# Differential attention in 16 groups: one unrolled sequence, three score banks, maxima of two heads at once

## The reference

```python
qkv = x @ Wqkv                                     # x: normalised and modulated rows
q = qkv[..., :2 * Hx].reshape(Bx, 2 * NQ, Sx, HD)  # 32 query heads of 16, Sx = 2048
k = qkv[..., 2 * Hx:2 * Hx + G].reshape(Bx, NKV, Sx, HD)   # 8
v = qkv[..., 2 * Hx + G:].reshape(Bx, NKV, Sx, HD)
k = jnp.repeat(k, 2 * NQ // NKV, axis=1)
v = jnp.repeat(v, NQ // NKV, axis=1)
scores = jnp.einsum('bhqd,bhkd->bhqk', q, k) / math.sqrt(HD)
scores = jnp.where(causal, scores, -jnp.inf)
aw = jax.nn.softmax(scores, axis=-1)
aw = aw.reshape(Bx, NQ, 2, Sx, Sx)
aw = aw[:, :, 0] - lam * aw[:, :, 1]
attn = jnp.einsum('bhqk,bhkd->bhqd', aw, v) * (1.0 - LAMBDA_INIT)
```

## Time and profile before

| | |
|---|---|
| median of three runs | 2430.19 us (2429.91 to 2431.61) |
| the profiled execution | 2430.3 us |
| its span, first to last instruction | 2428.4 us |
| TensorE busy | 2220.2 us, 91% |
| VectorE busy | 1829.4 us, 75% |
| ScalarE busy | 1547.9 us, 64% |
| GpSimd busy | 525.7 us, 22% |
| granted TensorE clock, mean | 0.949 |

### The profile page before, as it was taken

How to read it: one execution, slowest core, us unless ns; L and a number is a source line. 1 busy time by engine, 2 the same in 40 slices (tenths; PEclk the granted TensorE clock), 3 DMA queues, 4 the chain that set the end, 5 groups by cost and what they waited for, 6 DMA issues and landing times. The chain is left out here.

```text
span 2428.4 us, 46606 instructions
## 1 busy us (share of the span) xinstructions
PE 2220.2 (91%) x17772; PEld 992.5 (41%) x17772; DVE 1829.4 (75%) x3782; ACT 1547.9 (64%) x3105; POOL 525.7 (22%) x584
## 2 busy tenths in 40 slices
PE   6799999999999999999999999999999979889984
PEld 4233333333333333333333333334333258567831
DVE  2788888878787888888888888887888348434467
ACT  2167677777767776767676777777767725235633
POOL 2112121303222121212121213131201014100067
PEclk8589999999999999999999999999999979899955
DMA  4120302121121202020303030212100030000001
GB/s 145 36 58 6 66 11 61 22 50 32 41 41 31 47 25 47 30 56 17 66 6 66 6 66 18 55 27 45 32 12 2 2 96 0 1 1 1 1 22 48
DMA packets 95990, 84.79 MB, mean 35 GB/s; under 512 B 48544, under 2 KB 81440, under 8 KB 95776
## 3 DMA queue, kind: packets, MB, share of 16 engines
q1 hardware_dynamic: 95776, 81.91, 15.2%
HBM read 26.81 MB, written 16.78 MB: 18 GB/s over the span
## 5 line engine op out<-in xcount | busy, mean ns | idle before, releaser
L605 DVE TENSOR_REDUCE m_part<-a_bank 128x1 f32<-128x512 f32 (+3 forms) x2560 | 1395.5, 603 | 270.0 <-PE a_bank L906 163.2
L749 ACT ACTIVATE probs<-b_bank 128x512 f32<-128x512 f32 (+1 forms) x2304 | 1173.2, 578 | 412.4 <-PE b_bank L922 407.2
L922 PE MATMUL b_bank<-q_pack,k_pack 34*128 34x512 bf16 (+7 forms) x5120 | 949.0, 348 | 6.2 <-DMA q_pack<-m_rows 1.8
L894 PE MATMUL a_bank<-k_pack,q_pack 64*128 64x512 bf16 (+3 forms) x2560 | 847.2, 357 | 58.5 <-DVE m_part L605 33.0
L960 PE MATMUL acc<-probs,v_tile 128*32 128x512 f32 (+3 forms) x5120 | 587.1, 540 | 22.6 <-ACT o_sb L756 21.5
L922 PEld LDWEIGHTS b_bank<-q_pack,k_pack 34*128 34x128 bf16 (+1 forms) x5120 | 316.5, 94 | 547.7 <-ACT probs L749 392.6
L894 PEld LDWEIGHTS a_bank<-k_pack,q_pack 64*128 64x128 bf16 x2560 | 238.2, 94 | 333.4 <-DVE m_part L605 255.2
L476 POOL TENSOR_SCALAR_AFFINE_SELECT probs<-probs 128x512 f32<-128x512 f32 (+1 forms) x192 | 151.5, 789 | 1019.4 <-ACT probs L749 1019.4
L906 PE MATMUL a_bank<-future,pick 64*128 64x128 bf16 x2048 | 278.3, 219 | 0.0
L906 PEld LDWEIGHTS a_bank<-future,pick 64*128 64x128 bf16 x2048 | 185.7, 96 | 47.5 <-issue 4.7
L960 PEld LDWEIGHTS acc<-probs,v_tile 128*32 128x32 f32 x5120 | 107.3, 108 | 186.6 <-issue 94.2
(11 more groups left out here) (193 smaller groups left out, 1761.0 us busy)
## 6 DMA issues: line engine op xcount, KB each, us to landing
q_pack<-part SPq DMA_DIRECT2D x384, 64.0 KB, 2.3
k_pack<-part SPq DMA_DIRECT2D x192, 64.0 KB, 2.3
scratch<-qkv_row SPq DMA_DIRECT2D x16, 512.0 KB, 2.8
heads<-scratch SPq DMA_DIRECT2D x16, 512.0 KB, 3.7
xg<-in_L_attn_x SPq DMA_DIRECT2D x16, 256.0 KB, 2.8
scratch<-qkv_row SPq DMA_DIRECT2D x32, 128.0 KB, 2.7
q_pack<-m_rows SPq DMA_DIRECT2D x256, 2.0 KB
x<-in_L_attn_x SPq DMA_DIRECT2D x4, 1024.0 KB, 11.7
```

Of the source, the lines that this page charges most:

```text
L605: dve.tensor_reduce(m_part[:, 2 * hp + side, t, c:c + 1], a_bank[at % A_RING][:, 0:width_a(u % UNITS)], AX.X, ALU.max).then_inc(a_maxed, 1)
L749: act.activation(probs[:, s % P_RING, h, at:C], b_bank[bank_no(("B", par, s, h))][:, at:C], ACT.Exp, scale=HD ** -0.5) \
L894: ins = pe.matmul(a_bank[at % A_RING][:, 0:w], q_pack[buf][rows, hp, 0, q:q + P], k_pack[buf][rows, 0, C * c:C * c + w], start=True, stop= ...
L922: ins = pe.matmul(b_bank[bank_no(slot)][:, at:at + C - q], k_pack[par][rows, n2, P * kt:P * (kt + 1)], q_pack[par][rows, h // 2, n2, C * j ...
```

## The change

- One list over all 16 x 36 steps (TAIL steps with three more at the end) takes the place of the list for two groups. The flush is gone: the last two `meet_v` of a group fall into steps 0 and 1 of the next, the copy of `acc` into step 1 and piece O into step 2.
- `b_bank` has three banks. The slots of a step are now h0, h1, extra pieces, h2, h3. The extra pieces stand between the two `two_heads`, on TensorE behind `meet_v` and on ScalarE between the exponentials of h1 and h2; so do ScalarE's copies.
- `a_bank` has two pairs of banks. A unit waits for the reduction of the unit two before it; VectorE reduces both heads in one instruction, when both are scored. The masks of a unit with fewer than 512 columns come one score earlier.
- The output: ScalarE copies the turned rows to `o_rows`, VectorE takes reciprocal and signs one step later, GpSimd scales and adds.
- VectorE's negation of a block's maxima is spread over the next two units; piece M comes one step later; T0 to T3 come one step later; the gather of heads goes from VectorE (step 15) to GpSimd (step 14).

```diff
...
 SIDES = (1, 0)
-A_RING = 3
-B_RING = 4
+A_RING = 2
+B_RING = 3
...
-PREP_AT = {7: "N", 8: "W0", 9: "W1", 10: "W2", 11: "W3", 17: "T0", 18: "T1", 19: "T2", 20: "T3"}
...
+PREP_AT = {7: "N", 8: "W0", 9: "W1", 10: "W2", 11: "W3", 18: "T0", 19: "T1", 20: "T2", 21: "T3"}
+COPY_AT = {STEPS * g + J_LAST[j] + LAG: 4 * g + j for g in range(GROUPS) for j in range(NJ)}
+OUTPUT_AT = {n + 1: block for n, block in COPY_AT.items()}
+MAXIMA_AT = {n + 2: 4 * (u // UNITS) + A_LAST.index(u % UNITS)
+             for n in range(LAST_STEP) for u in units(n) if u % UNITS in A_LAST}
+GATHER_AT = 14
...
-SLOTS = [slot for par in range(2) for s in range(STEPS)
-         for slot in [("B", par, s, h) for h in range(QH)] + [(use, par, s, 0) for use in MISC[s]]]
-SLOTS[-1:-1] = [None] * (-len(SLOTS) % B_RING)
+TAIL = LAST_STEP + LAG + 1
+USES = [use for n in range(TAIL) for use in uses_at(n)]
+SLOTS = [slot for n in range(TAIL)
+         for slot in [("B", n, h) for h in range(QH // 2) if n < LAST_STEP] + uses_at(n)
+         + [("B", n, h) for h in range(QH // 2, QH) if n < LAST_STEP]]
+SLOT_NO = {slot: at for at, slot in enumerate(SLOTS)}
...
-        a_bank = [ps(f"a_bank{i}", [P, C]) for i in range(A_RING)]
+        a_bank = [ps(f"a_bank{i}", [P, 2, C]) for i in range(A_RING)]
         b_bank = [ps(f"b_bank{i}", [P, C]) for i in range(B_RING)]
...
+            def gather_heads(n):
+
+                pool.wait_ge(heads_in, 32 * (n + 1))
+                pool.wait_ge(turned, 4 * n)
+                pool.tensor_copy(heads_by_j[:, :, :, :], heads[:, :, :].rearrange("p h (j d) -> p j h d", d=HD)) \
+                    .then_inc(heads_ready, 1)
...
+            def pair(n):
+
+                g, j = n // NJ, n % NJ
+                o = o_sc[:, :].rearrange("p (t h e) -> p t h e", t=TB, h=QH)
+                halves = o_sc[:, :].rearrange("p (t a c e) -> p t a c e", t=TB, a=2, c=2)
+                dst = attn[:, g, TB * j:TB * (j + 1), :].rearrange("p t (a e) -> p t a e", a=2)
+                pool.wait_ge(o_weighed, n + 1)
+                if n:
+                    pool.wait_ge(o_added, n)
+                pool.tensor_tensor(o, o_rows[:, :].rearrange("p (t h e) -> p t h e", t=TB, h=QH)[:, :, :, 0:HD],
+                                   o_w[:, :, :].unsqueeze(3).broadcast_to([P, TB, QH, HD]), ALU.mult).then_inc(o_scaled, 1)
+                pool.wait_ge(o_scaled, n + 1)
+                pool.tensor_tensor(dst, halves[:, :, :, 0, :], halves[:, :, :, 1, :], ALU.add).then_inc(o_added, 1)
...
-            def maximum(i, par, u):
+            def maximum(u):

                 j, t, c, hp = A_UNITS[u % UNITS]
-                for n, side in enumerate(SIDES):
-                    at = 2 * a_count(i, par, u) + n
-                    dve.wait_ge(a_scored, at + 1)
-                    dve.tensor_reduce(m_part[:, 2 * hp + side, t, c:c + 1], a_bank[at % A_RING][:, 0:width_a(u % UNITS)],
-                                      AX.X, ALU.max).then_inc(a_maxed, 1)
-
-            def negate(i, par, u, j, m):
-
-                dve.wait_ge(a_maxed, 2 * a_count(i, par, u) + 2)
-                dve.tensor_reduce(m_max[:, :, :], m_part[:, :, :, 0:j + 1], AX.X, ALU.max).then_inc(m_step, 1)
-                dve.wait_ge(m_step, upto(2 * m + 1))
-                if not (isinstance(m, int) and m == 0):
-                    dve.wait_ge(m_copied, upto(m))
+                dve.wait_ge(a_scored, 2 * u + 2)
+                dve.tensor_reduce(m_part[:, j % 2, 2 * hp:2 * hp + 2, t, c], a_bank[u % A_RING][:, :, 0:width_a(u % UNITS)],
+                                  AX.X, ALU.max).then_inc(a_maxed, 1)
...
-            def weigh(i, par, last, s, j):
-
-                n = 4 * (2 * i + par) + j
-                o = b_bank[bank_no((f"O{j}", par, s, 0))][:, :].rearrange("p (t h e) -> p t h e", t=TB, h=QH)
-                dve.wait_ge(misc_filled, upto(misc_no(i, par, last, s, f"O{j}")))
-                dve.reciprocal(o_rl[:, :, :], o[:, :, :, HD]).then_inc(o_step, 1)
-                dve.wait_ge(o_step, upto(2 * n + 1))
-                dve.tensor_tensor(o_w[:, :, :], o_rl[:, :, :], signs[:, :, :], ALU.mult).then_inc(o_step, 1)
-                dve.wait_ge(o_step, upto(2 * n + 2))
-                dve.wait_ge(o_added, upto(START + n - (1 if par or j else 0)))
-                dve.tensor_tensor(o_sc[:, j % 2, :].rearrange("p (t h e) -> p t h e", t=TB, h=QH), o[:, :, :, 0:HD],
-                                  o_w[:, :, :].unsqueeze(3).broadcast_to([P, TB, QH, HD]), ALU.mult).then_inc(o_scaled, 1)
...
+            def invert(n):
+
+                dve.wait_ge(o_taken, n + 1)
+                if n:
+                    dve.wait_ge(o_scaled, n)
+                dve.reciprocal(o_rl[:, :, :], o_rows[:, :].rearrange("p (t h e) -> p t h e", t=TB, h=QH)[:, :, :, HD]) \
+                    .then_inc(o_inverted, 1)
+
+            def weigh(n):
+
+                dve.wait_ge(o_inverted, n + 1)
+                dve.tensor_tensor(o_w[:, :, :], o_rl[:, :, :], signs[:, :, :], ALU.mult).then_inc(o_weighed, 1)
...
-            def body(i, last):
-                for par in range(2):
-                    g = 2 * i + par
-                    for s in range(STEPS):
-                        exponentials(i, par, s)
-                        for j in range(NJ):
-                            if s == J_LAST[j] + LAG or s == STEPS - 1 == J_LAST[j]:
...
+            def take_rows_of_output(block, no, bank):
+                act.wait_ge(misc_filled, no)
+                if block:
+                    act.wait_ge(o_added, block)
+                act.activation(o_rows[:, :], bank[:, :], ACT.Copy).then_inc(o_taken, 1)
+
+            for n in range(TAIL):
+                if n < LAST_STEP:
+                    for h in range(QH // 2):
+                        exponential(n, h)
+                if n in COPY_AT:
+                    take_output(COPY_AT[n])
+                for use in uses_at(n):
+                    (what, k), no, bank = use, use_no(use), b_bank[bank_no(use)]
+                    if what == "N":
+                        shift_rows(k, no, bank)
+                    if what == "W":
+                        take_rows(k // 4, k % 4, no, bank)
+                    if what == "T":
+                        take_heads(k // 4, k % 4, no, bank)
+                    if what == "M":
+                        take_maxima(k, no, bank)
+                    if what == "O":
+                        take_rows_of_output(k, no, bank)
+                    if what == "T" and k % 4 == 3:
+                        first_part(k // 4)
+                if n < LAST_STEP:
+                    for h in range(QH // 2, QH):
+                        exponential(n, h)
         @block.tensor
...
+            def wait_for_bank(slot):
+
+                if SLOT_NO[slot] >= B_RING:
+                    was = SLOTS[SLOT_NO[slot] - B_RING]
+                    if was[0] == "B":
+                        pe.wait_ge(b_exped, START + QH * was[1] + was[2] + 1)
+                    else:
+                        emptied(*was)
...
-                at = 2 * a_count(i, par, u) + n
                 rows = slice(HALF * side, HALF * (side + 1))
-                if at >= A_RING:
-                    pe.wait_ge(a_maxed, at - A_RING + 1)
-                ins = pe.matmul(a_bank[at % A_RING][:, 0:w], q_pack[buf][rows, hp, 0, q:q + P], k_pack[buf][rows, 0, C * c:C * c + w],
+                if n == 0 and u >= A_RING:
+                    pe.wait_ge(a_maxed, u - A_RING + 1)
+                ins = pe.matmul(a_bank[u % A_RING][:, side, 0:w], q_pack[buf][rows, hp, 0, q:q + P], k_pack[buf][rows, 0, C * c:C * c + w],
...
-            def body(i, last):
-                for par in range(2):
-                    g = 2 * i + par
-                    for s in range(STEPS):
-                        j = B_STEPS[s][0]
-                        if s == J_FIRST[j]:
-                            pe.wait_ge(m_rows_in, upto(16 * QH * (4 * g + j + 1)))
-                        ahead = [u for u in units(s) if not (last and par == 1 and u >= UNITS)]
-                        ending = s == STEPS - 1
-                        pieces = 2 + (LAG if ending else 0)
-
...
-                        if UNITS in ahead:
-                            pe.wait_ge(packs_in, 16 * PACK_DMAS * (g + 2))
-                        two_heads(i, par, s, 0, maxima(0), last)
-                        if s >= LAG:
-                            meet_v(i, par, s - LAG)
-                        two_heads(i, par, s, 1, maxima(1), last)
-                        if ending:
-                            for k in range(LAG):
-                                for u in maxima(2 + k):
-                                    score_maxima(i, par, u)
...
+            for n in range(TAIL):
+                g, s = n // STEPS, n % STEPS
+                ahead = list(units(n)) if n < LAST_STEP else []
+                if n < LAST_STEP and s in J_FIRST:
+                    pe.wait_ge(m_rows_in, 16 * QH * (NJ * g + J_FIRST.index(s) + 1))
```

(59 more changed lines are left out.)

343 lines of the change are left out of this document (138 added, 205 removed).

## The result

The changed kernel takes 2534.6 us (median of four, 2533.3 to 2537.2), the kernel before 2430.05 in the same batch: a ratio of 1.0426, 95% interval 1.0411 to 1.0442. It is slower by 104 us; forecast were 72, in a range that held it. The profiled execution took 2533.4 us, its span is 2531.7 at a mean granted clock of 0.947 (before: 0.949).

The account below looks back on a forecast made before the run. TensorE was taken to set the pace at 2.50 us a step, VectorE close behind. 14 groups x 4.4 + 2 + 10 - 3 + 1 gave +72 on 2430.3, so 2502 us; range 2395 to 2560, one in ten beyond each end.

Parts of the forecast that it names:

- the price that decides: Three score banks, not four: h1's scores wait for the exponential of h2, plain steps 2.82 us instead of 2.50.
- Rival (a): Faster: the three-bank loop is not felt, -3.6 us a group, 2375 us; chance 0.12.
- Rival (b): Faster: VectorE sets the time and 1280 fewer reductions count in full, 2390 or 2248 us; chance 0.08.
- (d): Nothing moves: the flush and copies give what the loop costs, 2425 to 2435 us; chance 0.07.
- Rival (c): Slower still: later rows and paired reductions feed each other's waits, 122.5 to 123 a group, 2550 to 2560 us; chance 0.15.
- Group 15 longest in relation: Sign in the profile after: the last group, 92.03 us before, would take 102.1, +10.
- A gap of 2 us after the split: Sign in the profile after: TensorE idle 2 us behind ScalarE's 1.91 us split.
- the wait for the rows: Step 10 waits for its maxima rows: some 4.5 us in group 14, 0.6 to 0.7 in a group with preparation.
- Cost 0; were that cover gone, T0 would wait 1 to 2 us: Moving the output's rescaling and the gather of heads from VectorE to GpSimd would cost nothing.
- the pairs of maxima: Units waiting for paired reductions hold up h1 after steps with three or four units: 3.5 us a group.
- A TensorE that waits mainly for the paired reductions: Sign in the profile after that would show the forecast wrong; no size given.
- The lead: The 46 units ahead of the loop, VectorE's alone, would get 3 us shorter.

Follow-up runs that it names:

- the best kernel: Changed kernel with four score banks, three single maxima banks, GpSimd's split held until step 27's exponentials, maxima rows ahead of pack transfers: 2398.9 us, ratio 0.9860.

## Why the prediction was right, and where its sum was off

**Right: the price that decides.** The loop 1.29 + 0.22 + 0.32 + 1.00 was forecast at 2.82 a step, and it is 2.82 in the changed kernel, in the old one with three banks, and in the new one with single maxima banks; 2.50 with four; 2.61 with half of h2's exponential. Rival (a), in which the loop is not felt, is out. Rival (b) is out by the 142 us less of VectorE that brought nothing, and (d) by 104 us. Rival (c), 2550 to 2560, came nearer to 2534.6 than the 2502 did, but not by its causes: no wait for rows in a usual group, and little cost of the pairs. "Group 15 longest in relation": 12%, forecast 102.1, measured 103.7. "VectorE below 90": 88.0. "A gap of 2 us after the split" on ScalarE: the score behind it waits 1.82 us:

```profile
1416.23 1.91 ACT L718 ACTIVATE part<-headT 80x2048 bf16<-80x2048 f32 x1
...
1418.67 0.39 PE L913 MATMUL b_bank<-q_pack,k_pack 64*128 64x512 bf16 x1 [1.82 <-ACT probs L746]
```

**Right in group 14: the wait for the rows.** Forecast 4.5, measured 3.8 at step 10, which took 7.37 there (before: 1.84). The group as a whole came out at 114.6 and not 110.4: behind the wait the granted clock was 0.58 from 1859.90 to 1866.19 us, a cost that the sum did not have. The answer on the bank's loads (idle us, times):

```profile
  DMA q_pack<-m_rows: 3.8, 1
```

The 0.7 us forecast for each other group (its own times, 33.8 less 33.3, give 0.5) did not show in group 10: step 10 was 0.57 shorter than forecast. I had the time of arrival and the time of need each to a microsecond, and their difference is no better than that.

**Off: a usual group +6.7 to +7.2, not +4.4.** In group 10 the steps come to 121.6, 2.2 above the forecast (119.4 with its steps rounded one by one):

- Step 26, +1.0 in five of the groups. The failing sentence is "Cost 0; were that cover gone, T0 would wait 1 to 2 us". I asked only who waits for the rescaling on GpSimd and not what the signs' product, still on VectorE, meets there. The product runs into the split, and the reductions stand behind it. The kernel before had shown 0.92 for a product of 0.17.
- In the other nine groups step 26 is as forecast and the loss sits in steps 22 and 23, 9.33 us in group 8 for 8.14 in group 10 (some 8.3 by the prediction's terms). The sum had the gap behind the split on ScalarE, and nothing for what the gap can do to the granted clock, which falls to 0.51 behind it.
- Steps 3, 21 and 19, +1.6 (0.88, 0.56, 0.18). The negation, spread over two more units, comes late, and TensorE's turn of maxima waits for it, 21.1 us in all, where the kernel before shows one wait of 0.4. I costed it at nothing and never named its cover. The wait in step 3:

```profile
1350.55 0.22 PE L827 MATMUL b_bank<-identb,m_neg 128*32 128x128 bf16 x1 [0.72 <-DVE m_neg L607]
```

- Steps 30 and 6, +0.46, with no cause followed up.
- Against these steps 10, 20 and 2, -1.2: the rows' wait and ScalarE's copies were overestimated there.
- The rest is spread over steps at 0.1 to 0.3 each.

**Right sum, wrong ground: the pairs of maxima.** The steps for which I put down 3.5 us came out within 0.2 each, yet single maxima banks give nearly the same steps. So the pairs' own price was mis-sized: 0.9 us for four steps and not 2.95. With single maxima these four steps take the same with three score banks as with four (4.49, 3.36, 3.14, 3.50), so what is left in them is the third unit itself, on TensorE and VectorE, which no run separates. "A TensorE that waits mainly for the paired reductions" was to prove me wrong and does not appear: 166.4 + 78.3 us of loads and matmuls, where the single ones had 255.2 + 33.0 before:

```profile
PEld a_bank L882 <- DVE m_part L589: 166.4, 251, 1.7
...
PE a_bank L882 <- DVE m_part L589: 78.3, 143, 1.1
```

**A size that I forecast wrongly.** The waits of the scores for the exponentials were to rise by 8 us a group, some 120; they rose from 392.6 (655) to 448.7 (742). The pieces take part in the same rotation of banks now and wait too:

```profile
PEld b_bank L832 <- ACT probs L746: 50.1, 59, 1.5
...
PEld b_bank L827 <- ACT probs L746: 34.2, 61, 1.0
...
PEld b_bank L814 <- ACT probs L746: 32.0, 56, 0.8
PEld b_bank L822 <- ACT probs L746: 30.1, 42, 0.8
```

The four together are 146 us, where the pieces of the kernel before waited 11 us for exponentials. With the 56 of the scores that is some 190 more; in part they may be the old gaps of the queue under a new name, which was not separated, so they can't be added to the loss.

**The lead** gave 7.4 us and not 3. The end gave 0.1 and not +1.

**Where the 104 us come from**, as far as shown: the fourth bank 88 to 90. With four banks and single maxima the new order costs 32 us, and gives 21 once the split is held back. Three banks and pairs together soften that collision (step 26 3.81 or 2.83 and not 6.51), and behind a long wait the clock can fall or not, so the parts don't add up. The forecast of 72 held its range by the one price that decides; the collision and the clock, some 1 to 1.2 us a group, were in it only through the width of the range.

## What to carry to other kernels

Before a bank is taken away, write down for each use which earlier reader it then waits for, and compare the way from that fill to the release (here 1.29 us) with the distance in the queue (0.88). Keep small VectorE instructions with two SBUF inputs away from long GpSimd ones, above all where something on the path stands behind them. A place in the list of an engine that otherwise idles fixes an order and no time: it runs ahead until a wait holds it. Behind a long wait of TensorE, read the granted clock as well: the steps there can grow although nothing in them waits.

## What the runs showed of the hardware

Small instructions of VectorE from SBUF to SBUF were held up to the end of a GpSimd elementwise operation if they began even 0.20 us behind it: 0.17 to 3.40 us (product), 0.16 to 3.89 (negation with two inputs), and 2.15 for one with a single input, 128x16 f32 to bf16. The last I had not expected; the Trainium skill ("SBUF — State Buffer", "Who interferes with whom") counts this kind of instruction among those that can, by their operands, take the port pair shared with GpSimd, and the trace agrees. GpSimd's masks hold them up too: 0.91 and 1.08 us beside masks of 1.10. Reductions from PSUM stay at 1.22 us beside the same operations. A start decides by hundredths: 0.02 us behind GpSimd's the negation took 0.16 and GpSimd's paid, with 0.07; 0.03 behind it, in the best kernel's group 12, it took 4.07.

TensorE's granted clock fell from 1.00 to about 0.50 behind single waits in an otherwise busy engine: 1.82 us (nine groups of 14 in the changed kernel), 2.46 us (with four banks), 3.15 us (split held back, three banks) and 3.50 us (rows of group 14). It did not fall behind the 1.82 us of the other five groups, nor behind the 1.84 us of group 14 in the kernel before. While it was down, matmuls of 512 columns stood 0.42 us apart and not 0.22.
